# A two-layer attention kernel: layer 1's first projections and rotations as work items of layer 0's last steps, and scores and maxima in strict turns

## Chip, cores and metric

The kernel runs on one core of a Trainium2 chip. The metric is the device time of one launch in microseconds. TensorE is called PE here (PEld: its weight loads), VectorE DVE, ScalarE ACT, GpSimd POOL, and SyncE, which issues the DMAs, SP.

## What is computed

Two layers on x of 2 x 1024 rows of 128 (float32), each `x = x + attention(norm(x)) + ffn(norm(x))`:

```
# layer 0: 16 heads of 8, ALiBi and causal mask, softmax
att = softmax(q @ k.T / sqrt(8) + slope * (j - i), causal);  y = (att @ v) @ W_proj + b_proj
# layer 0 ffn: second normalisation, input quantised by one global maximum, ternary weight
xq = clip(xn2 * 128 / gamma); y = (xq @ w_q) * (gamma * beta / 128)
# layer 1: 16 query heads of 64 over 4 key heads, rotary embedding, linear attention
q, k = rope(xn @ Wq.T), rope(xn @ Wk.T)
per chunk: o = ((q k^T) * decay) v + (q * q_dec) state;  state = blk_dec * state + (k * k_dec)^T v
# layer 1 ffn: linear plus top-2 of 8 experts of rank 4
```

`rope(x) = x * cos + rotate_half(x) * sin`.

## The kernel before

**Layer 0.** Groups of four heads, eight groups (two batches by four), ten steps each: steps 0 to 79. Step `s` has unit `u = s % 10` of group `n = s // 10`: a block of scores up to 512 columns wide for each of four heads (256 in u = 2 and 9), its exponential on ACT (line 1480), the zeroing of the upper triangle in diagonal blocks on POOL (`affine_select`, 1620), and one step later the product with V (`pv`, 721), which adds in PSUM bank 7. ACT copies the sum to `yacc` twice in a group (1469). Scores rotate over three banks (`ST_BANKS`), so that a head's score waits for the exponential of the head three before.

**Items.** The softmax needs the row maxima of the same scores one group ahead. For each group there are 18 maxima items: PE makes a block of scores for a pair of heads (`max_piece`, 591, one product in rows 0 to 63 of the array and one in rows 64 to 127 for the two heads, in up to two pieces, and `max_done`, 605, which adds the causal mask by 64 x 64 products in nine of eighteen or so), DVE reduces (1170). All items share two pairs of banks: item k waits until item k - 2 has been used (`used(pe, k - 2)`). `item_stream` lists the items in order, `MIDWAY` puts those of the attention's finish between the maxima, and `TAIL` gives those after the last maxima a step of their own. `items_of_step(s)` deals two paced items to a step. Per step PE runs, for each half (heads 0, 1, then 2, 3): scores and half of the items, and after both halves `pv(s - 1)`. DVE runs the step's items in their order, and after them what is put at that step by name: `LN1_STEP` (moments, inverse root and normalisation of batch 0 for layer 1: one after the item `back` of span 1), `QUANTISE_STEP`, `ternary` and so on.

**The finish** of a span of 512 rows is `yt` (two a span, heads back to rows and division), `yT`, `proj` (659, 661: ffn product and projection in one bank, DVE adds the bias, 1183), `back` (665, DVE adds to x, 1220); then `xn1T` turns the normalised rows of batch 0 for layer 1 (680, 1192). Before the change these fall in steps 42, 45, 49, 52 (`yt`), 56, 59 (`yT`), 68, 71 (`proj`), 72, 73 (`back`), 76 (`xn1T`); the normalisation is at step 74.

**Hand-over.** Spans 2 and 3 (batch 1) are finished after step 79 by the list `POST`: eight `turn_heads` (800), `yT`, `proj`, `back`. The ten projections of layer 1's first span (`("p", 0, m)`: two of keys, eight of queries, 836) stand between them. A projection is rotated so: DVE multiplies by cos (1313) into `kr` or `qr`, and by sin (1317) into one of three slots of `by_sin`; SP waits for it and issues two DMAs (521) that swap odd and even rows into one of four slots of `turned`; POOL adds that to `kr` or `qr` (1641). After POST: `chunk_vk(0)` (844, 847), ACT's copy of `vk` and eight `vdec` (1501, 1512), `scores1(0)` (865), which needs the rotated keys and queries, then per chunk `kv_sums` (919), the next span's projections, `mix` (889) and `carry` (906).

Of `scores_beside`, which the change rewrites, this is the core before:

```
for odd in (1, 0):
    scores(s, [heads[1 - odd]])
    if odd:
        used(pe, k - 2)
        max_ready(k)
    for t in range(len(ROUNDS[...])):
        last = max_piece(k, t, odd)
max_done(k, last)
```

Of the kernel before, what the change touches and what calls it, by code (L numbers as in the profile page):

```python
# [78 lines left out]
for _name, _n in [("cos", T), ("sin", T), ("decay", H1 * D1), ("qdec", QT * P), ("kdec", H1),  # L79
# [67 lines left out]
ITEM_AT_TURN = TURN_AT[0, 0]  # L147
ITEM_AT = {(kind, n): k for k, (kind, n, u) in enumerate(ITEMS) if u == 0}
# [29 lines left out]
QUANTISE_STEP = [63, 65]  # L178
# [4 lines left out]
def build(nc, x, w, wright, consts, alibi_q, alibi_k, masks, chosen, out):  # L183
    alibi_q, alibi_k, masks, chosen = (v.bitcast(BF16) for v in (alibi_q, alibi_k, masks, chosen))
    with ExitStack() as ctx:
# [71 lines left out]
        qr = sb("qr", [P, 2, QT, SPAN], F32, l1)
        kr = sb("kr", [P, 2, 2, SPAN], F32, l1)

        apart = sb("apart", [P, 6 * T], F32, l1)  # L260
        qd = sb("qd", [P, 2, QT, P], F32, l1)
        state = sb("state", [P, STATES, QT, D1], F32, l1)
# [102 lines left out]
        POST = []  # L365
# [6 lines left out]
        PJ = [("p", 0, m) for m in range(PROJ)]  # L372
# [68 lines left out]
        def _(sp):  # L441
# [69 lines left out]
            def turn_halves(i, ms):  # L511
# [27 lines left out]
        def _(pe):  # L539
# [32 lines left out]

            def max_ready(k):
# [21 lines left out]
            def max_done(k, last):  # L595
# [16 lines left out]
            def scores_beside(s, heads, k):  # L612
                for odd in (1, 0):
                    scores(s, [heads[1 - odd]])
                    if odd:
                        used(pe, k - 2)
                        max_ready(k)
                    for t in range(len(ROUNDS[MAX_OF[ITEMS[k][2]][1]])):
                        last = max_piece(k, t, odd)
                max_done(k, last)  # L620

            def item(k):
# [20 lines left out]
                elif kind != "turn":  # L643
# [129 lines left out]
            for s in range(NSTEP + 1):  # L773
                beside = items_of_step(s) if s < NSTEP else ()
                for half in range(2):
                    mine = (beside[:(len(beside) + 1) // 2], beside[(len(beside) + 1) // 2:])[half]
                    if s < NSTEP:
# [4 lines left out]
                        else:  # L782
                            scores(s, heads)
# [46 lines left out]
            def project1(i, ms):  # L830
# [3 lines left out]
                for m in ms:  # L834
                    w = W["k1"][:, P * m:P * m + P] if m < 2 else W["q1"][:, P * (m - 2):P * (m - 2) + P]
                    mm(bank01(("p", i, m)), w, xnT[:, SPAN * i:SPAN * i + SPAN], start=True, stop=True).then_inc(s_pj, 1)  # L836

            def chunk_vk(c):
# [7 lines left out]
                for pr in range(2):  # L846
                    last = tr(ps[:, KV1 * D1 + P * pr:KV1 * D1 + P * pr + P], kr[:, i % 2, pr, P * ch:P * ch + P], W["ident"])  # L847
# [3 lines left out]
            def scores1(c):  # L851
# [5 lines left out]
                for pr in range(2):  # L857
# [158 lines left out]
        def _(v):  # L1016
# [231 lines left out]
            def after_attention():  # L1248
                v.wait_ge(s_big, 48)
                for name in POST:  # L1250
# [49 lines left out]
            def rope(i, ms):  # L1300
# [3 lines left out]
                for m in ms:  # L1304
                    n = PROJ * i + m
# [5 lines left out]
                    t = slice(SPAN * (i % 2), SPAN * (i % 2) + SPAN)  # L1311
                    dst = kr[:, i % 2, m, :] if m < 2 else qr[:, i % 2, m - 2, :]
                    note(vec.tensor_tensor(dst, ps, K["cos"][:, t], ALU.mult))  # L1313
                    if n >= SIN_SLOTS:
                        q, slot = divmod(n - SIN_SLOTS, TURN_SLOTS)
                        v.wait_ge(s_turned[slot], 32 * (q + 1))
                    vec.tensor_tensor(by_sin[:, n % SIN_SLOTS, :], ps, K["sin"][:, t],  # L1317
                                      ALU.mult).then_inc(free(("p", i, m)), 1)
# [8 lines left out]
            def fade_q(c):  # L1327
# [4 lines left out]
                vec.tensor_tensor(qd[:, c % 2, :, :], qr[:, i % 2, :, P * ch:P * ch + P],  # L1332
# [228 lines left out]
        def _(g_):  # L1561
# [46 lines left out]

            for s in range(NSTEP):
# [22 lines left out]

            def rotate(i, ms):

                if i == NSPAN:
                    return
                for m in ms:
                    n = PROJ * i + m
                    g_.wait_ge(s_turned[n % TURN_SLOTS], 32 * (n // TURN_SLOTS + 1))
# [130 lines left out]
```

## Time and profile before

| | us |
|---|---|
| median of three runs (lowest, highest) | 517.77 (517.55, 519.68) |
| the profiled execution | 513.83 |
| its span | 512.0 |
| mean granted clock | 0.944 |

The profile tells of one execution. Times of instructions are from the start of its span. The granted clock is a share of 2.4 GHz: 1.00 or 0.50 at a time, in between over a longer stretch. A releaser behind `<-` is what ended an engine's idle time, and the idle time stands before it.

### The profile page before, as it was taken

Reading aid. Unit: us, or ns where it says so; the run is one execution under the profiler, and the core shown is the slowest. Engines: PE = TensorE matmul, PEld = TensorE weight load, DVE = VectorE, ACT = ScalarE, POOL = GpSimd, SP = SyncE. Lnnn points to the kernel's source line nnn. Section 1 sums busy time; section 2 is a strip of 40 time slices with the busy share of each in tenths; the row PEclk is TensorE's granted clock in tenths of the full one; section 3 lists DMA queues with packets and bytes.
Section 4 is the critical chain, followed back from the end, with each engine's and each line's share of the span. In section 5 each row is a group of like instructions: output and inputs, shape, how many; then the busy total and the mean of one; then the engine's idle time right before and its main releaser. Section 6 shows DMA issues by size and latency. Waiting matters only on the chain. (4 is left out here: it accounts for less than half of the span.)

```text
span 512.0 us, 10900 instructions
## 1 busy us (share of the span) xinstructions
PE 434.6 (85%) x4283; PEld 199.5 (39%) x4284; DVE 354.2 (69%) x612; ACT 264.9 (52%) x593; POOL 183.6 (36%) x277
## 2 busy tenths in 40 slices
PE   6797989898998989998886796959698769889995
PEld 3253223232332323332221342426274526446764
DVE  5878778878898788888825485885908690777351
ACT  2566387877776677768577212435313530453331
POOL 3013425354322204132220165649307830685220
PEclk9999599999999899999999897987989997998999
DMA  7542070424202020020000031220102210120000
GB/s 238 191 125 71 8 241 2 173 50 170 70 3 69 2 59 14 3 70 2 2 3 2 10 139 57 104 73 32 63 22 79 69 61 22 63 83 2 3 22 22
DMA packets 19094, 31.95 MB, mean 62 GB/s; under 512 B 2544, under 2 KB 7120, under 8 KB 18724
## 3 DMA queue, kind: packets, MB, share of 16 engines
q1 hardware_dynamic: 19044, 31.27, 18.8%
q8 instruction: 34, 0.56, 0.4%
q14 instruction: 16, 0.13, 0.1%
HBM read 13.23 MB, written 8.06 MB: 42 GB/s over the span
## 5 line engine op out<-in xcount | busy, mean ns | idle before, releaser
L1170 DVE TENSOR_REDUCE pmax<-PS 128x8 f32<-128x1024 f32 x144 | 170.7, 1220 | 39.0 <-PE PS L605 30.0
L1480 ACT ACTIVATE prob<-PS 128x512 f32<-128x512 f32 (+1 forms) x320 | 158.3, 560 | 68.8 <-PE PS L703 67.0
L703 PE MATMUL PS<-q_op,k_op 55*128 55x512 bf16 (+3 forms) x384 | 93.0, 335 | 12.4 <-ACT prob L1480 10.0
L1620 POOL TENSOR_SCALAR_AFFINE_SELECT prob<-prob 128x512 f32<-128x512 f32 x64 | 39.9, 635 | 165.2 <-ACT prob L1480 165.2
L591 PE MATMUL PS<-k_op,q_op 52*128 52x512 bf16 (+3 forms) x384 | 80.1, 343 | 11.6 <-DVE pmax L1170 8.6
L721 PE MATMUL PS<-prob,vaug 128*16 128x512 f32 (+3 forms) x768 | 81.1, 512 | 1.8 <-ACT prob L1480 1.8
L703 PEld LDWEIGHTS PS<-q_op,k_op 55*128 55x128 bf16 x384 | 26.1, 95 | 87.9 <-ACT prob L1480 69.6
L1658 POOL TENSOR_TENSOR xn<-state,c_sb 128x512 f32<-128x512 f32 x28 | 32.1, 1147 | 77.7 <-DVE state L1350 69.0
L836 PE MATMUL PS<-xnT,w_sb 128*128 128x512 f32 x80 | 43.9, 648 | 14.4 <-DVE by_sin L1317 14.4
L1350 DVE TENSOR_TENSOR state<-PS,xn 128x512 f32<-128x512 f32 x28 | 19.3, 688 | 45.7 <-PE PS L919 34.1
L1641 POOL TENSOR_TENSOR qr<-qr,turned 128x512 f32<-128x512 f32 x32 | 43.0, 1361 | 5.0 <-DMA turned<-by_sin 4.9
L937 PE MATMUL PS<-oT,w_sb 128*128 128x256 f32 (+1 forms) x160 | 33.5, 372 | 1.2 <-ACT oT L1547 1.2
L1547 ACT COPY oT<-PS 128x512 f32<-128x512 f32 x32 | 17.2, 588 | 32.6 <-PE PS L906 32.5
L591 PEld LDWEIGHTS PS<-k_op,q_op 52*128 52x128 bf16 x384 | 21.7, 95 | 30.3 <-DVE pmax L1170 22.6
L1512 ACT ACTIVATE vdec<-vk,c_sb 128x64 f32<-128x64 f32 x128 | 32.3, 334 | 0.5
L1501 ACT COPY vk<-PS 128x512 f32<-128x512 f32 x16 | 9.3, 584 | 44.0 <-PE PS L847 44.0
L937 PEld LDWEIGHTS PS<-oT,w_sb 128*128 128x128 f32 x160 | 28.4, 210 | 8.6 <-issue 3.7
L1317 DVE TENSOR_TENSOR by_sin<-PS,c_sb 128x512 f32<-128x512 f32 x40 | 27.1, 679 | 0.0
L1313 DVE TENSOR_TENSOR qr<-PS,c_sb 128x512 f32<-128x512 f32 x32 | 21.9, 684 | 7.5 <-PE PS L836 7.4
L865 PE MATMUL PS<-qr,kr 64*64 64x256 f32 x256 | 19.7, 416 | 8.6 <-POOL qr L1641 8.6
L1324 DVE TENSOR_TENSOR sm<-PS,c_sb 128x512 f32<-128x512 f32 x32 | 20.5, 680 | 9.1 <-PE PS L865 9.1
L1332 DVE TENSOR_TENSOR qd<-qr,c_sb 128x1024 f32<-128x1024 f32 x16 | 24.8, 1547 | 0.0
(186 smaller groups left out, 533.7 us busy)
## 6 DMA issues: line engine op xcount, KB each, us to landing
turned<-by_sin SPq DMA_DIRECT2D x80, 128.0 KB, 2.0
k_op<-k_scr SPq DMA_DIRECT2D x14, 220.0 KB
q_op<-q_scr SPq DMA_DIRECT2D x14, 208.0 KB
c_sb<-const_dram SPq DMA_DIRECT2D x1, 2060.0 KB, 7.2
w_sb<-w_dram SPq DMA_DIRECT2D x1, 1876.5 KB, 7.8
q_scr<-part_a SPq DMA_DIRECT2D x6, 256.0 KB, 3.5
k_scr<-part_a SPq DMA_DIRECT2D x6, 256.0 KB, 3.7
q_scr<-part_b SPq DMA_DIRECT2D x6, 256.0 KB, 3.4
```

The lines of the kernel that those rows point to most:

```text
L591: return mm(PS[:, ring + odd, P * at:P * (at + nb)], q_op[rows, slot, pair, P * i:P * i + P], k_op[rows, slot, pair, P * j:P * (j + nb)], ...
L703: last = mm(PS[:, (GH * s + h) % ST_BANKS, at:at + nn], k_op[rows, slot, h // 2, P * j:P * j + P], q_op[rows, slot, h // 2, P * i0:P * i0 ...
L721: last = mm(PS[STRIP * h:STRIP * h + VW, 7, c0:c0 + nn], vaug[:, TPB * b + j, g * GH + h, :], prob[:, s % P_SLOTS, h, at:at + nn], start=( ...
L836: mm(bank01(("p", i, m)), w, xnT[:, SPAN * i:SPAN * i + SPAN], start=True, stop=True).then_inc(s_pj, 1)
L937: last = mm(of_half(ps, s), wo[:, C * kt:C * kt + C], of_half(oT[:, i % 2, kt, :], s), start=False, stop=(chunks.stop == TPS and s == 1 an ...
L1170: vec.tensor_reduce(pmax[:, of_pair, at:at + TPS], both.rearrange("p a (b c) -> p a b c", c=P), AX.X, ALU.max).then_inc(done, 1)
L1317: vec.tensor_tensor(by_sin[:, n % SIN_SLOTS, :], ps, K["sin"][:, t], ALU.mult).then_inc(free(("p", i, m)), 1)
L1480: sca.activation(prob[:, s % P_SLOTS, h, 0:UNIT_W[u]], PS[:, k % ST_BANKS, 0:UNIT_W[u]], ACT.Exp).then_inc(s_exp, 1)
L1512: sca.mul(vdec[:, c % 2, g, h % HPG, :], vk[:, c % 2, D1 * g:D1 * g + D1], K["kdec"][:, h:h + 1]).then_inc(s_vd_a, 1)
L1620: po.affine_select(out=blk, in_=blk, compare_op=ALU.is_ge, fill=0.0, base=0, pattern=[[0, GH], [1, P]], channel_multiplier=-1).then_inc(s_ ...
L1641: po.tensor_tensor(dst, dst, turned[:, n % TURN_SLOTS, :], ALU.add).then_inc(done, 1)
L1658: po.tensor_tensor(faded, state[:, u % STATES, :, :], fade, ALU.mult).then_inc(s_faded, 1)
```

## The change

Nothing of what is computed changes. Five things are altered.

1. The finish of batch 0 is placed earlier. By `item_stream` the steps are now: `yt` 42, 44, 46, 47; `yT` 49, 51; `proj` 52, 54; `back` 56, 57; `xn1T` 63. `LN1_STEP` follows `back` of span 1: step 58. `QUANTISE_STEP` is 48 and 50, not 63 and 65.
2. A new item `p1` makes two projections of layer 1's first span into the two banks of the item's pair, and DVE multiplies both by cos and sin. The five stand in steps 70, 72, 73, 75 and 76. SP waits for the item; POOL adds the swapped rows at the end of steps 72, 74, 75, 77, 78, after that step's `affine_select`. `POST` holds no projection any more.
3. `scores_beside`: the second head's score comes after all products of the maximum, masks included; these alternate between the two halves of the array's rows.
4. In other steps the two heads of a half have their scores one after the other, each with its own wait.
5. `qr` and `kr` are two tensors each, and the buffers of layer 1 lie in another order, so that the first span's and `by_sin` and `turned` can be written while layer 0 still runs.

```diff
+APART = 6848
-TAIL = [(71, "proj", 1, 0), (72, "back", 0, 0), (73, "back", 1, 0), (76, "xn1T", 0, 0)]
-MIDWAY = {(5, 5): ("yt", 0, 0), (5, 11): ("yt", 0, 1), (6, 0): ("yt", 1, 0), (6, 6): ("yt", 1, 1),
-          (6, 12): ("yT", 0, 0), (7, 0): ("yT", 1, 0), (7, 17): ("proj", 0, 0)}
+MIDWAY = {(5, 6): ("yt", 0, 0), (5, 9): ("yt", 0, 1), (5, 12): ("yt", 1, 0), (5, 15): ("yt", 1, 1),
+          (6, 0): ("yT", 0, 0), (6, 3): ("yT", 1, 0), (6, 6): ("proj", 0, 0), (6, 9): ("proj", 1, 0),
+          (6, 12): ("back", 0, 0), (6, 15): ("back", 1, 0), (7, 8): ("xn1T", 0, 0)}
+TAIL = [(70, "p1", 0, 0), (72, "p1", 0, 1), (73, "p1", 0, 2), (75, "p1", 0, 3), (76, "p1", 0, 4)]
+TURN_STEP = {72: 0, 74: 1, 75: 2, 77: 3, 78: 4}
...
-QUANTISE_STEP = [63, 65]
+QUANTISE_STEP = [48, 50]
...
-        for i, ms in zip(SECOND, (range(0, 3), range(0))):
-            POST += [("yt", i, g) for g in range(NG)] + [("p", 0, m) for m in ms]
         i, j = SECOND
-        POST += [("yT", i), ("p", 0, 3), ("p", 0, 4), ("proj", i), ("yT", j), ("p", 0, 5), ("back", i), ("p", 0, 6),
-                 ("proj", j), ("p", 0, 7), ("back", j), ("p", 0, 8), ("p", 0, 9)]
+        POST = [("yt", i, g) for g in range(NG)] + [("yt", j, g) for g in range(NG)]
+        POST += [("yT", i), ("proj", i), ("yT", j), ("back", i), ("proj", j), ("back", j)]
...
-                    freed(sp, ("p", i, m))
+                    if i:
+                        freed(sp, ("p", i, m))
+                    else:
+                        used(sp, P1_AT[m // 2])
...
-                        for odd in range(2):
+                        for odd in (1, 0):
                             rows = slice(HALF * odd, HALF * odd + HALF)
...
             def scores_beside(s, heads, k):
-                for odd in (1, 0):
-                    scores(s, [heads[1 - odd]])
-                    if odd:
-                        used(pe, k - 2)
-                        max_ready(k)
-                    for t in range(len(ROUNDS[MAX_OF[ITEMS[k][2]][1]])):
+                scores(s, heads[0:1])
+                used(pe, k - 2)
+                max_ready(k)
+                for t in range(len(ROUNDS[MAX_OF[ITEMS[k][2]][1]])):
+                    for odd in (1, 0):
                         last = max_piece(k, t, odd)
                 max_done(k, last)
+                scores(s, heads[1:2])
...
+                    elif kind == "p1":
+                        pe.wait_ge(s_big, 48)
+                        used(pe, ITEM_AT["xn1T", 0])
+                        for m in (2 * u, 2 * u + 1):
+                            last = mm(o[:, m % 2, :], weights_of(m), xnT[:, 0:SPAN], start=True, stop=True)
...
-                            scores(s, heads)
+                            for h in heads:
+                                scores(s, [h])
...
+                elif kind == "p1":
+                    v.wait_ge(s_big, 48)
+                    for m in (2 * u, 2 * u + 1):
+                        ins = rotated(0, m, both[:, m % 2, :])
...
+            def rotated(i, m, ps):
+                n = PROJ * i + m
+                t = slice(SPAN * (i % 2), SPAN * (i % 2) + SPAN)
+                dst = kr[i % 2][:, m, :] if m < 2 else qr[i % 2][:, m - 2, :]
+                note(vec.tensor_tensor(dst, ps, K["cos"][:, t], ALU.mult))
+                if n >= SIN_SLOTS:
+                    q, slot = divmod(n - SIN_SLOTS, TURN_SLOTS)
+                    v.wait_ge(s_turned[slot], 32 * (q + 1))
+                return vec.tensor_tensor(by_sin[:, n % SIN_SLOTS, :], ps, K["sin"][:, t], ALU.mult)
...
+                if s in TURN_STEP:
+                    rotate(0, range(2 * TURN_STEP[s], 2 * TURN_STEP[s] + 2))
...
-            rotate(0, range(PROJ))
```

## Rows read from the trace of the kernel before

**Rows 1.** The page, part 1: busy us, share of the span, instructions.
```profile
PE 434.6 (85%) x4283; PEld 199.5 (39%) x4284; DVE 354.2 (69%) x612; ACT 264.9 (52%) x593; POOL 183.6 (36%) x277
```
**Rows 2.** Stages: length, busy PE, PEld, DVE, ACT, POOL, PEclk, DMA share, GB/s.
```profile
82.40:106.00 23.60, 21.60 (x207) 6.57 (x202) 19.67 (x18) 19.34 (x40) 9.76 (x21) 1.00 0.37 121
169.20:175.10 5.90, 4.89 (x37) 1.69 (x37) 3.18 (x4) 3.43 (x8) 1.25 (x3) 0.71 0.01 2
314.00:326.00 12.00, 12.00 (x113) 5.58 (x110) 9.94 (x15) 3.53 (x11) 4.45 (x5) 0.82 0.17 61
```
**Rows 3.** Timeline, steps 16 and 17: start, length, instruction, idle before.
```profile
97.95 0.39 PE L703 MATMUL PS<-q_op,k_op 55*128 55x512 bf16 x1
...
99.41 0.11 PEld L605 LDWEIGHTS PS<-masks_sb 64*64 64x64 bf16 x4 [0.23 <-issue]
...
100.57 0.39 PE L703 MATMUL PS<-q_op,k_op 55*128 55x512 bf16 x1
...
101.25 2.36 DVE L1170 TENSOR_REDUCE pmax<-PS 128x8 f32<-128x1024 f32 x2 [0.26 <-PE PS L591]
...
102.03 1.05 PE L721 MATMUL PS<-prob,vaug 128*16 128x512 f32 x8
...
103.01 0.33 PE L703 MATMUL PS<-q_op,k_op 55*128 55x384 bf16 x1
```
**Rows 4.** The page, part 5: busy, mean ns, idle before, most of it for.
```profile
L1170 DVE TENSOR_REDUCE pmax<-PS 128x8 f32<-128x1024 f32 x144 | 170.7, 1220 | 39.0 <-PE PS L605 30.0
L1480 ACT ACTIVATE prob<-PS 128x512 f32<-128x512 f32 (+1 forms) x320 | 158.3, 560 | 68.8 <-PE PS L703 67.0
```
**Rows 5.** Timeline of the hand-over.
```profile
287.17 0.58 ACT L1469 COPY yacc<-PS 128x512 f32<-128x512 f32 x1 [2.58 <-PE PS L721]
...
288.81 0.26 DVE L1212 RECIPROCAL rden<-PS 128x16 f32<-128x16 f32 x1 [11.12 <-PE PS L800]
...
312.98 1.13 PE L865 MATMUL PS<-qr,kr 64*64 64x256 f32 x8 [3.70 <-POOL qr L1641]
...
314.03 0.30 PEld L919 LDWEIGHTS PS<-vdec,vk 64*64 64x64 f32 x8 [0.74 <-POOL vdec L1649]
```
**Rows 6.** Timeline, first and last part of the normalisation on DVE.
```profile
267.63 1.64 DVE L1039 BATCH_NORM_STATS2 stats<-x_sb 128x6 f32<-128x128 f32 x8
...
273.08 2.14 DVE L1058 TENSOR_SCALAR xn<-x_sb,mv,rstd 128x128 f32<-128x128 f32 x8
```
**Rows 7.** Timeline, items of the finish in steps 71, 73 and 76.
```profile
259.97 1.12 PE L659 MATMUL PS<-xn2T,w_sb 128*128 128x512 f32 x2
...
261.89 0.39 PE L703 MATMUL PS<-q_op,k_op 55*128 55x384 bf16 x4
...
266.14 0.66 PE L665 MATMUL PS<-w_sb,sT 128*128 128x128 f32 x4
...
276.47 1.22 DVE L1192 COPY xnT<-PS 128x1024 f32<-128x1024 f32 x1 [1.25 <-PE PS L680]
```
**Rows 8.** Timeline of steps 40 and 41.
```profile
167.15 0.28 DVE L1140 TENSOR_SCALAR xn<-w_sb,small 128x128 f32<-128x128 f32 x1
...
169.79 0.39 PE L687 MATMUL PS<-masks_sb,mpart 128*12 128x128 bf16 x4 [0.83 <-DVE pmax L1170]
...
171.74 1.91 PE L721 MATMUL PS<-prob,vaug 128*16 128x512 f32 x8
```
**Rows 9.** Timeline of steps 75 to 79.
```profile
272.20 0.39 PE L703 MATMUL PS<-q_op,k_op 55*128 55x512 bf16 x2 [0.83 <-ACT prob L1480]
...
275.37 1.06 PE L680 MATMUL PS<-w_sb,xn 128*128 128x128 f32 x8 [1.47 <-DVE xn L1058]
...
282.99 1.22 POOL L1620 TENSOR_SCALAR_AFFINE_SELECT prob<-prob 128x512 f32<-128x512 f32 x2 [1.90 <-ACT prob L1480]
...
284.67 0.63 POOL L1620 TENSOR_SCALAR_AFFINE_SELECT prob<-prob 128x512 f32<-128x512 f32 x1 [0.46 <-ACT prob L1480]
```
**Rows 10.** The tile `turned`: length ns min/median/max; DMAs to landing.
```profile
L521 SPq DMA_DIRECT2D turned<-by_sin x80: 464/590/1474, 292.6 to 454.8; - x80
L1641 POOL TENSOR_TENSOR kr<-kr,turned x8: 1267/1271/1280, 295.3 to 442.0; 128x512 f32<-128x512 f32 x8
...
DMA to landing us min/median/max: 1.9/2.0/3.7
```

More of the change, by code:

```diff
@@ L147 @@
 ITEM_AT_TURN = TURN_AT[0, 0]
+P1_AT = {u: k for k, (kind, n, u) in enumerate(ITEMS) if kind == "p1"}
 ITEM_AT = {(kind, n): k for k, (kind, n, u) in enumerate(ITEMS) if u == 0}
@@ L253, in build @@
         sm = sb("sm", [P, 4, SPAN], F32, l1)
+        qr1, kr1 = sb("qr1", [P, QT, SPAN], F32, l1), sb("kr1", [P, 2, SPAN], F32, l1)
+        state = sb("state", [P, STATES, QT, D1], F32, l1)
+        apart = sb("apart", [P, APART], F32, l1)
+        qd = sb("qd", [P, 2, QT, P], F32, l1)
+        qr0, kr0 = sb("qr0", [P, QT, SPAN], F32, l1), sb("kr0", [P, 2, SPAN], F32, l1)
         by_sin = sb("by_sin", [P, SIN_SLOTS, SPAN], F32, l1)
         turned = sb("turned", [P, TURN_SLOTS, SPAN], F32, l1)
[L257 to L262, printed above, removed]
+        qr, kr = (qr0, qr1), (kr0, kr1)
         l1.close()
@@ L363, in build @@
             RA += [("yT", i), ("proj", i)]
-        POST = []
-        for i, ms in zip(SECOND, (range(0, 3), range(0))):
-            POST += [("yt", i, g) for g in range(NG)] + [("p", 0, m) for m in ms]
         i, j = SECOND
-        POST += [("yT", i), ("p", 0, 3), ("p", 0, 4), ("proj", i), ("yT", j), ("p", 0, 5), ("back", i), ("p", 0, 6),
-                 ("proj", j), ("p", 0, 7), ("back", j), ("p", 0, 8), ("p", 0, 9)]
-        PJ = [("p", 0, m) for m in range(PROJ)]
+        POST = [("yt", i, g) for g in range(NG)] + [("yt", j, g) for g in range(NG)]
+        POST += [("yT", i), ("proj", i), ("yT", j), ("back", i), ("proj", j), ("back", j)]
+        PJ = []
         NORM_CHUNK, TURN_CHUNK = 1, 3
@@ L571, in _, with weights_of @@
             pe.wait_ge(s_masks, 16)
+            def weights_of(m):
+                return W["k1"][:, P * m:P * m + P] if m < 2 else W["q1"][:, P * (m - 2):P * (m - 2) + P]
             def max_ready(k):
@@ L834, in project1 @@
                 for m in ms:
[L835 to L836 removed]
+                    mm(bank01(("p", i, m)), weights_of(m), xnT[:, SPAN * i:SPAN * i + SPAN], start=True, stop=True).then_inc(s_pj, 1)
             def chunk_vk(c):
@@ L846, in chunk_vk @@
                 for pr in range(2):
-                    last = tr(ps[:, KV1 * D1 + P * pr:KV1 * D1 + P * pr + P], kr[:, i % 2, pr, P * ch:P * ch + P], W["ident"])
+                    last = tr(ps[:, KV1 * D1 + P * pr:KV1 * D1 + P * pr + P], kr[i % 2][:, pr, P * ch:P * ch + P], W["ident"])
                 last.then_inc(s_pj, 1)
@@ L865, in scores1 @@
                             last = mm(PS[half_of(s), 2 + q, 256 * pr:256 * pr + 256].rearrange("p (a t) -> p a t", a=HPG),
-                                      kr[rows, i % 2, pr, t], qr[rows, i % 2, HPG * pr:HPG * pr + HPG, t],
+                                      kr[i % 2][rows, pr, t], qr[i % 2][rows, HPG * pr:HPG * pr + HPG, t],
                                       start=True, stop=True, skip_group_check=True)
@@ L1185, in item @@
                     add_to_x(n, both[:, 0, :]).then_inc(done, 1)
+                elif kind == "p1":
+                    v.wait_ge(s_big, 48)
+                    for m in (2 * u, 2 * u + 1):
+                        ins = rotated(0, m, both[:, m % 2, :])
+                        if m % 2 == 0:
+                            note(ins)
+                    ins.then_inc(done, 1)
                 elif kind == "lanes":
@@ L1310, in rope @@
                         v.wait_ge(s_sc, 2 * TPS * (i - 1))
[L1311 to L1318, printed above, removed]
+                    rotated(i, m, ps).then_inc(free(("p", i, m)), 1)
             def masked(c, q):
@@ L1331, in fade_q @@
                     v.wait_ge(s_o, 2 * (c - 1))
-                vec.tensor_tensor(qd[:, c % 2, :, :], qr[:, i % 2, :, P * ch:P * ch + P],
+                vec.tensor_tensor(qd[:, c % 2, :, :], qr[i % 2][:, :, P * ch:P * ch + P],
                                  K["qdec"].rearrange("p (k t) -> p k t", k=QT), ALU.mult).then_inc(s_qd, 1)
@@ L1607, in normalise_again, with rotate @@
                 po.tensor_scalar(xn[:, j, :], xn[:, j, :], rstd2[:, j:j + 1], None, ALU.mult).then_inc(s_xn2, 1)
+            def rotate(i, ms):
+                if i == NSPAN:
+                    return
+                for m in ms:
+                    n = PROJ * i + m
+                    g_.wait_ge(s_turned[n % TURN_SLOTS], 32 * (n // TURN_SLOTS + 1))
+                    dst, done = (kr[i % 2][:, m, :], s_kr) if m < 2 else (qr[i % 2][:, m - 2, :], s_qr)
+                    po.tensor_tensor(dst, dst, turned[:, n % TURN_SLOTS, :], ALU.add).then_inc(done, 1)
             for s in range(NSTEP):
@@ L1631, in _ @@
             po.memset(state[:, 0, 0, :], 0.0).then_inc(s_zero, 1)
[L1633 to L1639, printed above, removed]
-                    dst, done = (kr[:, i % 2, m, :], s_kr) if m < 2 else (qr[:, i % 2, m - 2, :], s_qr)
-                    po.tensor_tensor(dst, dst, turned[:, n % TURN_SLOTS, :], ALU.add).then_inc(done, 1)
             def fade_v(c):
```

5 lines of the change are left out of this document (removed).

## The prediction

> **What bounds the kernel now.** Order of reading: busy shares and costly groups of the page, a stretch of clean steps, one step at close range, then the places that the diff touches. By the page PE is busy 85% and DVE 69% [rows 1]; neither is a bound by itself. In 82.4 to 106.0, nine clean steps of layer 0, PE has 21.60 us of work in 23.6, DVE 19.67, ACT 19.34 [rows 2].
>
> The close view of steps 16 and 17 [rows 3] shows a loop, not a full engine: score of head 0 at 100.57, its exponential, head 3's score when that has freed a bank, P·V at 102.03, and head 0 of the next step at 103.01: 2.44 us. Step 16 (97.95 to 100.57), with a mask product between head 3's score and P·V, is 2.62: the mask costs 0.18. DVE needs 2.36 for a step's two maxima, ACT about 2.1 for four exponentials and up to 0.6 more where it copies. So a step has three limits close together. The page says the same: ACT stands idle 68.8 us before exponentials, nearly all for scores, and DVE 39.0 before maxima, 30.0 of it for items that end in a mask [rows 4].
>
> After layer 0 it is a chain: the last accumulator copy starts at 287.17 (0.58 long) and layer 1's first state product at 314.03, 26.3 us after the copy's end [rows 5]. In it lie eight head turns, ten projections and their rotations on DVE, SP's queue and POOL.
>
> **1. The normalisation at step 58.** It follows `back` of span 1, now an item of step 57. The block runs on DVE from 267.63 to 275.22 without a break, 7.6 us [rows 6]. There it hid beside an idle DVE; at 58 it stands ahead of the maxima of steps 59 and 60, and PE can be only two items ahead (the item pair of banks). By step 17's spacing, DVE is done with an item about 0.7 us before PE asks for its banks: 7.6 - 0.7 = 6.9 us of stall. Bounds: 7.6 (no slack), and 3.3, if DVE regains its idle time of the clean stretch (3.9 us in nine steps, 4.3 by step 68). I take 6.9, since two items are all that the banks hold.
>
> **2. The rest of batch 0's finish, in steps 42 to 63.** New in loaded steps are the second `proj`, two `back` and `xn1T`. `proj` holds PE from 259.97 to 261.89, 1.92 us; `back` 0.66 and some 0.3 of change around it; `xn1T` has 1.22 on DVE, where little room is left [rows 7]. I take 1.9 + 2 x 0.95 + 1.0 = 4.8; bounds 2.3 (each fills idle time of 0.8, as PE has in the last steps) and 6. The head turns, `yT`, the first `proj` and both quantising passes move among steps of equal load: 0, bounds -1 and +1.5.
>
> **3. PE's clock after the stall.** The nearest row is a small one: in step 40 a DVE chain of 1.4 us from 167.15 makes PE wait 0.83 for it, and then the clock is 0.71 over 5.9 us, which is half speed for 3.4 of them; P·V takes 1.91 instead of 1.05 [rows 2, 3, 8]. Half speed for 3.4 us loses 1.7, with the waits it moves 2.0. A hole of 7 us is larger than that one. I take +2.0, bounds 0 and 4. The Trainium skill (TensorE: Matmul & The Clock Gate, "The HAM clock gate") says that the chip gates PE's clock to half after idleness and releases it under work. By that rule the drop is certain, by the row it is likely; the term is the same.
>
> **4. Strict turns.** Where a half's first item is a maximum, all its products and masks now stand ahead of the second head's score. So the second item's masks leave the stretch from head 3 to P·V, 0.18 in steps 1, 5, 6, 8 and 9 of ten, but DVE (2.36) and ACT take over close behind: 0.1 in some 30 steps, -3. Against that, the first item's masks (steps 0, 2, 3 and 9) put the second head's score from 0.2 to about 0.7 us after the first, and ACT could be 0.2 late where it has no slack: 15 steps x 0.1, +1.5. I take -1.5, bounds -6 (0.1 in nearly all 66 steps) and +5 (0.2 in 26 steps). A mask's loads stand 0.23 behind the products before them [rows 3]. The Trainium skill (TensorEngine Tiling (Array Packing), "Key Properties") says that a change of tiling mode drains the engine. By that rule a mask ahead of head 3 adds a change back, and this term would be about +1.
>
> **5. Steps 70 to 79.** Five `p1` items, each two fp32 products as `proj` has: 1.92. PE stands idle 0.83 before the second pair of scores in a plain step [rows 9], so each adds 1.1: +5.5. Gone are `proj` and two `back` (1.92 + 2 x 0.66, less 0.83 in two steps: 1.6) and `xn1T` with its wait for the normalisation (1.06 + 1.47 - 0.83 = 1.7 [rows 9]), and in plain steps each head's score now waits for itself, 0.1 x 7. Net +1.5. The transfers: SP issues twenty at 0.59 in 25 us, behind nothing but the last `mrow` loads, 2.0 to landing [rows 10]. DVE has four operations, 2.5 us, an item, less than such a step is long, beside idle time. If that cover fails (three slots of `by_sin`, each freed by a landing), the steps wait: bounds -1 and +6.
>
> **6. POOL at the end.** The rotations of projections 8 and 9 stand at step 78, after its fills. DVE ends item 4 some 3.5 us after step 76 starts; the transfers land 2.7 and 4 us later; POOL adds twice, 1.27 each [rows 10], between the fills of step 78 (282.99, 1.22) and that of 79 (284.67) [rows 9], on which P·V waits. Fill 79 could have started 0.4 to 0.8 after those of 78; behind 2.5 it is 1.7 late: +1.7, bounds 0 and 3.
>
> **7. Hand-over.** Left after the last copy: eight head turns (DVE from 1.1 us after the copy [rows 5], 0.62 each, done after 6.1), then `yT`, `proj`, `sT`, `back` for two spans, interleaved, one after another's product at 0.6, 1.0, 0.7, 0.6 and 0.7 for the addition: 12.0. Then `vk` 1.0, its copy 0.6, eight `vdec` 2.0 and semaphores: the state product 15.9 after the copy, not 26.3: -10.4. The wait of 3.70 for POOL's rotated queries [rows 5] is gone too; late next is ACT's `vdec`. Bounds -8 and -13. In 314 to 326 the clock is 0.82, half speed for 4.3 us, behind that wait [rows 2]; if PE's holes shrink, up to 2.2 comes back: I take -1.0.
>
> Sum: 6.9 + 4.8 + 2.0 - 1.5 + 1.5 + 1.7 - 10.4 - 1.0 = +4.0. The profiled execution took 513.83 (span 512.0), so one like it would take 517.8; the median of the runs is 517.77, 3.94 more, and 4.0 on that is 521.8.
>
> **Rivals.** *DVE is fed early and catches up* (faster). If strict turns hand it the second maximum ahead of head 3's wait in every step, the 39 us of idle time before maxima [rows 4] shrink, part 4 is -4.5, DVE regains 3.6 of the block at 58, and PE's hole is too short for the clock: 4.0 - 3.0 - 3.6 - 2.0 = -4.6, 513.2. It decides where that idle time falls under half. Against it: the loop of 2.44 holds no maximum.
> *The clock stays up* (no change): no drop at 59, and strict turns give 2.5 more: 4.0 - 2.0 - 2.5 = -0.5, 517.3. For it: clock stretches depend on where in a pause they fall. Against: step 40.
> *The rotation ring holds the last steps* (slower still): DVE waits in `by_sin` for a landing, the item banks stay full, part 5 is at its bound of +6: 526.3. For it: the same ring fills in the hand-over now. Against: mostly two steps between items.
> That the projections do not leave the hand-over is excluded: no wait ties the items to the last copy.
>
> Chances: forecast 0.43, ring 0.12, clock up 0.23, DVE catches up 0.22. A measurement tells 0.5%, 2.6 us, from no change. So slower 0.55, same 0.23, faster 0.22. Range 511 to 528, the forecast's own 519 to 525.
>
> **What would show it.** Right: DVE's block at step 58 with a hole of 6 to 7 us in PE and a stretch at half clock behind it; the last copy about 15 us later than now; the state product some 16 us after it. Wrong: no hole in steps 59 to 61; clean steps below 2.4; the last copy before 295, or the state product 20 or more behind it.

## The result, and the profile after

The changed kernel takes 538.0 us (median of four runs, 532.79 to 540.18), the one before 517.66 (four runs, 514.21 to 519.68): ratio 1.045, interval 1.040 to 1.050. The direction was as forecast, the size was not: +4 forecast, 20 to 23 measured, and outside the range. Time below is compared by ratio where experiments are set against each other; 1% is 5.16 us. A ratio, and a half-speed time below, is taken over the runs within 1.5% of the fastest of their kernel, a median over all of its runs, and the two differ by up to 0.6% (this kernel is at 1.045 by the first and at 1.039 by the second, or 1.043 against 29 later runs of the kernel before).

The page of the changed kernel, beside [rows 1] and [rows 4]: busy times, the granted clock in 40 slices (before it was 0.944 in the mean, here 0.899), and the two groups of the layer 0 loop.
```profile
PE 460.7 (86%) x4283; PEld 206.9 (38%) x4284; DVE 355.7 (66%) x612; ACT 267.6 (50%) x593; POOL 184.8 (34%) x277
...
PEclk9997599959999698897698978796989997998999
...
L1501 ACT ACTIVATE prob<-PS 128x512 f32<-128x512 f32 (+1 forms) x320 | 160.1, 559 | 95.1 <-PE PS L718 93.9
L1183 DVE TENSOR_REDUCE pmax<-PS 128x8 f32<-128x1024 f32 x144 | 171.2, 1221 | 53.7 <-PE PS L615 42.2
```
PE is busy 26 us longer with as many instructions (4283), while ACT and DVE have the same work and more idle time, most of it for PE. So PE ran slower: the clock, not more work on another engine.

Stages of the changed kernel, cut at the first exponential of steps 4, 19, 41, 49, 60, 69, 70 (columns as in [rows 2]). The windows begin at those steps and end at steps 19, 23, 43, 52, 64, 70 and 79.
```profile
67.17:105.77 38.60, 36.42 (x336) 10.98 (x336) 31.67 (x29) 31.79 (x66) 13.82 (x29) 1.00 0.37 123
105.77:124.20 18.43, 17.12 (x128) 5.96 (x128) 9.91 (x11) 8.42 (x19) 7.72 (x17) 0.63 0.23 79
175.96:187.78 11.82, 10.52 (x65) 3.73 (x65) 6.48 (x10) 4.03 (x10) 3.25 (x9) 0.57 0.00 1
206.46:220.52 14.06, 11.96 (x100) 4.47 (x98) 11.10 (x13) 7.10 (x14) 5.36 (x11) 0.76 0.01 2
247.21:270.45 23.24, 16.00 (x116) 4.90 (x116) 16.90 (x38) 9.52 (x20) 4.00 (x10) 0.63 0.01 2
282.90:288.05 5.15, 2.60 (x25) 1.04 (x26) 0.40 (x2) 1.77 (x6) 2.74 (x8) 0.85 0.01 2
288.05:316.39 28.34, 25.93 (x145) 7.59 (x145) 12.42 (x20) 19.03 (x39) 12.66 (x13) 0.97 0.25 94
```
The same cuts in the kernel before, without step 69:
```profile
67.42:106.07 38.65, 35.37 (x338) 10.71 (x337) 32.27 (x29) 31.31 (x66) 13.99 (x29) 1.00 0.38 127
106.07:118.17 12.10, 11.20 (x129) 4.78 (x129) 9.33 (x10) 7.73 (x19) 7.53 (x17) 1.00 0.10 22
169.18:177.99 8.81, 7.78 (x66) 2.94 (x66) 5.95 (x10) 4.21 (x10) 2.10 (x5) 0.81 0.00 1
194.59:203.45 8.86, 8.62 (x101) 3.73 (x98) 7.13 (x10) 6.30 (x15) 3.28 (x10) 1.00 0.01 2
228.01:238.67 10.66, 9.68 (x106) 3.25 (x103) 8.28 (x8) 8.53 (x20) 3.69 (x9) 1.00 0.00 1
257.75:283.11 25.36, 18.33 (x144) 5.89 (x144) 10.37 (x44) 19.47 (x39) 3.49 (x7) 1.00 0.01 2
```
At full clock the strict order changes nothing: steps 4 to 18 take 38.60, before 38.65. The last copy to `yacc` ends 35.1 us later than before (322.90 against 287.76). Of that, steps 60 to 63 give 12.6, steps 19 to 22 give 6.3 (equal work, clock 0.63 instead of 1.00), steps 49 to 51 5.2, steps 41 and 42 3.0, steps 70 to 78 3.0, the rest 5.0 together. Then the hand-over gives 8.8 back.

Timeline of the changed kernel: the normalisation, the hole, and what follows. Start, length, instruction, idle before.
```profile
245.08 1.65 DVE L1052 BATCH_NORM_STATS2 stats<-x_sb 128x6 f32<-128x128 f32 x8
...
250.54 2.14 DVE L1071 TENSOR_SCALAR xn<-x_sb,mv,rstd 128x128 f32<-128x128 f32 x8
...
253.87 0.61 PE L601 MATMUL PS<-k_op,q_op 52*128 52x256 bf16 x4 [6.76 <-DVE pmax L1183]
255.41 1.82 ACT L1501 ACTIVATE prob<-PS 128x512 f32<-128x512 f32 x3 [7.60 <-PE PS L718]
...
260.43 1.91 PE L736 MATMUL PS<-prob,vaug 128*16 128x512 f32 x8
```
The hole is there with the forecast length. But P·V still takes 1.91 instead of 1.05, and it starts 6.6 us after PE went on. A window of this kernel and one of the first experiment, which has the old order of products, both after the hole:
```profile
254.00:262.00 8.00, 8.00 (x53) 1.97 (x49) 4.56 (x4) 4.86 (x9) 1.43 (x3) 0.50 0.00 1
```
```profile
243.00:251.00 8.00, 7.83 (x71) 2.43 (x74) 5.18 (x5) 6.01 (x13) 2.13 (x4) 0.70 0.00 1
```
In the strict order PE is busy for all of 8 us and stays at 1.2 GHz; in the old order, no busier, it is back at 2.4 within them. The whole stretch at half clock runs from 249.0 to 266.0. It begins inside the hole, which starts at 247.1, and 12.1 us of PE's work lie in it:
```profile
249.00:266.00 17.00, 12.13 (x83) 3.27 (x83) 11.72 (x24) 6.27 (x13) 2.88 (x6) 0.50 0.01 2
```
In the first experiment it runs from 237.6 to 247.8, and PE goes on at 242.2: 5.6 us of it come behind the hole.

The hand-over of the changed kernel, beside [rows 5]:
```profile
317.98 2.49 POOL L1638 TENSOR_TENSOR qr<-qr,turned 128x512 f32<-128x512 f32 x2
320.43 0.64 POOL L1651 TENSOR_SCALAR_AFFINE_SELECT prob<-prob 128x512 f32<-128x512 f32 x1
321.21 1.05 PE L736 MATMUL PS<-prob,vaug 128*16 128x256 f32 x8 [1.14 <-POOL prob L1651]
322.32 0.58 ACT L1490 COPY yacc<-PS 128x512 f32<-128x512 f32 x1 [4.72 <-PE PS L736]
323.21 5.75 PE L816 MATMUL PS<-w_sb,yacc 128*128 128x128 f32 x32 [0.95 <-issue]
...
340.40 1.99 PE L934 MATMUL PS<-vdec,vk 64*64 64x256 f32 x16 [1.19 <-ACT vdec L1533]
```
The first state product comes 17.5 us after the copy's end, not 26.3. From there to the end nothing changes: 197.84 against 197.92.

### The profile page after: what moved, and what is told of

Read it like the earlier page. It is cut to its first block and busy times, and to the rows that moved or that the text cites. A ratio compares the mean times of both kernels' runs of the same rounds, so it can differ in the third digit from the quotient of the medians.

```text
span 538.2 us, 10867 instructions
## 1 busy us (share of the span) xinstructions
PE 460.7 (86%) x4283; PEld 206.9 (38%) x4284; DVE 355.7 (66%) x612; ACT 267.6 (50%) x593; POOL 184.8 (34%) x277
## 5 line engine op out<-in xcount | busy, mean ns | idle before, releaser
L1501 ACT ACTIVATE prob<-PS 128x512 f32<-128x512 f32 (+1 forms) x320 | 160.1, 559 | 95.1 <-PE PS L718 93.9
L1183 DVE TENSOR_REDUCE pmax<-PS 128x8 f32<-128x1024 f32 x144 | 171.2, 1221 | 53.7 <-PE PS L615 42.2
L718 PE MATMUL PS<-q_op,k_op 55*128 55x512 bf16 (+3 forms) x384 | 97.4, 355 | 5.8 <-ACT prob L1501 3.4
L601 PE MATMUL PS<-k_op,q_op 52*128 52x512 bf16 (+3 forms) x384 | 75.2, 361 | 17.4 <-DVE pmax L1183 13.3
L736 PE MATMUL PS<-prob,vaug 128*16 128x512 f32 (+3 forms) x768 | 86.8, 544 | 2.8 <-POOL prob L1651 2.8
L851 PE MATMUL PS<-xnT,w_sb 128*128 128x512 f32 x60 | 33.8, 663 | 13.6 <-DVE by_sin L1226 13.6
L601 PEld LDWEIGHTS PS<-k_op,q_op 52*128 52x128 bf16 x384 | 20.4, 98 | 34.1 <-DVE pmax L1183 22.9
L1672 POOL TENSOR_TENSOR vdec<-vk,c_sb 128x256 f32<-128x256 f32 x32 | 18.9, 611 | 28.2 <-ACT vk L1522 28.2
L736 PEld LDWEIGHTS PS<-prob,vaug 128*16 128x16 f32 x768 | 15.1, 99 | 32.1 <-issue 23.0
L1345 DVE TENSOR_TENSOR sm<-PS,c_sb 128x512 f32<-128x512 f32 x32 | 20.5, 683 | 6.5 <-PE PS L880 6.5
```

What stands on the lines that cost most here:

```text
L601: return mm(PS[:, ring + odd, P * at:P * (at + nb)], q_op[rows, slot, pair, P * i:P * i + P], k_op[rows, slot, pair, P * j:P * (j + nb)], ...
L718: last = mm(PS[:, (GH * s + h) % ST_BANKS, at:at + nn], k_op[rows, slot, h // 2, P * j:P * j + P], q_op[rows, slot, h // 2, P * i0:P * i0 ...
L736: last = mm(PS[STRIP * h:STRIP * h + VW, 7, c0:c0 + nn], vaug[:, TPB * b + j, g * GH + h, :], prob[:, s % P_SLOTS, h, at:at + nn], start=( ...
L851: mm(bank01(("p", i, m)), weights_of(m), xnT[:, SPAN * i:SPAN * i + SPAN], start=True, stop=True).then_inc(s_pj, 1)
L1183: vec.tensor_reduce(pmax[:, of_pair, at:at + TPS], both.rearrange("p a (b c) -> p a b c", c=P), AX.X, ALU.max).then_inc(done, 1)
L1501: sca.activation(prob[:, s % P_SLOTS, h, 0:UNIT_W[u]], PS[:, k % ST_BANKS, 0:UNIT_W[u]], ACT.Exp).then_inc(s_exp, 1)
```

## The experiments

"Half speed" is the time that PE had 1.2 GHz, worked out for each run as 2 x (1 - granted clock) x span, and averaged over a kernel's runs. The kernel before has 57.4 us of it in the 29 runs beside e1 to e4 (37.7 to 66.8), 57.2 beside e5 to e8 and 62.0 beside e9 to e12; the changed one has 99.6. The first number behind each experiment is its median. A ratio has an interval of about 0.5% either way, so a difference of two ratios is good to some 0.7%, or 4 us. "Strict order" is the order of the change's points 3 and 4.

**e1: the strict order undone.** The changed kernel with the three old places of order:
```
- scores(s, heads[0:1]); used(pe, k - 2); max_ready(k)
- for t in ...: for odd in (1, 0): ...
- scores(s, heads[1:2])
+ for odd in (1, 0):
+     scores(s, [heads[1 - odd]])
+     if odd: used(pe, k - 2); max_ready(k)
+     for t in ...
- for h in heads: scores(s, [h])
+ scores(s, heads)
```


> The changed kernel (median 538.0) with its scores and maxima back in the old order; everything else stays. Theory 'hole' (the normalisation's hole on the vector engine and the longer half-speed stretches behind it are the loss, strict turns are near nothing): 536 to 540, with the half-speed stretch of 17 us behind step 60 still there. Theory 'turns' (the new order starves PE, and causes the added half-speed stretches, as the one from 109.0 to 122.7): 526 to 531, total half-speed time down from 110 us to about 80. My estimate in the prediction was 1.5 us in favour of strict turns, so 539.5.


528.03, ratio 1.0235 (1.018 to 1.029), half speed 66.5. So 2.15%, 11 us, hangs on the order of the products (7 to 15 us with the noise of both).

**e2: the strict order alone.** The reverse edit in the kernel before.


> The kernel before (median 517.7) with strict turns alone. Theory 'hole': 515 to 519, and no more half-speed time than its 59 us. Theory 'turns': 523 to 528, with new half-speed stretches around steps 19 to 22 and 40 to 42.


519.92, ratio 1.0033 (0.999 to 1.008), half speed 59.9. Alone the strict order costs next to nothing (0.8% by the median). The two experiments contradict each other unless the order acts through something else in the changed kernel.

**e3: no normalisation at step 58.** Eight one-column operations stand in its place, so layer 1 reads an `xn` that is not the normalised one.
```
- moments(0); inverse_root(slice(0, TPB), 1e-5); normalise(0)
+ for j in range(TPB):
+     vec.tensor_scalar(xn[:, j, 0:1], x_sb[:, j, 0:1], 1.0, None, ALU.mult)
```


> The changed kernel with the normalisation block of step 58 left out (moments, inverse root, normalisation of batch 0 for layer 1; eight one-column operations stand in its place). Theory 'hole': PE's hole of 6.76 us is gone and with it the 17 us at half speed behind it; steps 60 to 63 last about 12 us, not 23.2: 524 to 528. Theory 'turns': only the hole goes, 531 to 533, since the slower clock has its cause elsewhere.


521.28, ratio 1.0044 (0.999 to 1.009), half speed 56.3. By the ratios the block costs 4.1% in strict order, 21 us, of which only 6.8 are the hole.

**e8: e3 with the old order.** It completes the square.


> The changed kernel in the old order of scores and maxima and with the normalisation block of step 58 left out (eight one-column operations in its place): what is left is the moved finish, p1 and the hand-over. If the two causes add (17 for the block, 10 for the order): 510 to 513. If they overlap, because the order only lengthens the half-speed stretch behind the hole: 518 to 521.


518.78, ratio 1.0050 (1.0015 to 1.009), half speed 58.0. The four corners, as ratios to the kernel before:

| | without the block | with it | the block costs |
|---|---|---|---|
| old order | e8 1.0050 | e1 1.0235 | 1.85%, 9.5 us |
| strict order | e3 1.0044 | changed kernel 1.0450 | 4.06%, 21 us |

By the ratios the order costs nothing without the block and 11 us with it, so that the two together cost more than their sum, by 11 us give or take 5. By the medians the corners are 1.006, 1.023, 1.010 and 1.039; the order then costs 2 us without the block and 8 with it.

The profiled executions say where. The windows of steps 60 to 63, here of e1 and then of e3:
```profile
235.58:256.19 20.61, 12.75 (x116) 4.49 (x116) 16.95 (x39) 9.27 (x20) 3.99 (x10) 0.75 0.01 2
```
```profile
240.83:253.31 12.48, 10.87 (x115) 4.11 (x112) 10.30 (x10) 9.11 (x19) 4.00 (x10) 1.00 0.01 2
```
With the hole in old order PE has 12.75 us of work for the same instructions that take 16.00 in strict order. The wait of the old order is the same, by the timeline of e1, and its P·V is at full speed 5.8 us after the products behind the hole:
```profile
242.24 0.62 PE L601 MATMUL PS<-k_op,q_op 52*128 52x256 bf16 x4 [6.75 <-DVE pmax L1182]
...
248.03 1.05 PE L736 MATMUL PS<-prob,vaug 128*16 128x512 f32 x8
```

In the four corners steps 60 to 63 take 12.38 (e8), 20.61 (e1), 12.48 (e3) and 23.24 us (changed kernel). In place, then, the block costs 8.2 us in the old order and 10.8 in the strict one, and the order makes 2.5 us of difference, not 11. The profiled executions of e1 and of the changed kernel are 11.5 us apart, and 11.7 of that stand ahead of the block: step 58 begins at 230.54 in e1 and at 242.22 in the changed kernel, and from there to the end they take 296.2 and 296.0. In e3 step 58 begins at 235.84. Nothing that DVE does in step 58 can act on the steps ahead of it, and there the changed kernel, e3 and e12 (below) are the same program. Their steps 19 to 57, in this order:
```profile
105.77:242.22 136.45, 124.06 (x1019) 42.74 (x1021) 103.63 (x125) 84.98 (x173) 34.78 (x80) 0.89 0.16 43
106.70:235.84 129.14, 115.67 (x1019) 40.48 (x1021) 103.14 (x125) 84.02 (x173) 34.21 (x80) 0.96 0.16 46
106.60:235.45 128.85, 114.36 (x1019) 39.91 (x1021) 103.00 (x125) 83.91 (x173) 34.23 (x80) 0.97 0.17 46
```
The same 1019 products take PE 8 to 10 us longer in one execution than in the others: 30.7, 10.2 and 6.8 us of these steps are at half clock. So a part of what separates these profiles is a difference between executions of the same code, in which the block has no hand that they show; how much of the 21 and the 11 us it makes cannot be told from one profile of each kernel. What goes with the order is more of such stretches: in steps 19 to 57 the five profiles with the strict order and the moved finish (changed kernel, e3, e4, e6, e12) have 6.8 to 30.7 us at half clock, the other nine 0 to 6.8.

**e6: only the halves without a maximum in the old order.** `for h in heads: scores(s, [h])` is `scores(s, heads)` again, the rest of the change stands.


> The changed kernel (538.0), where only the halves without a maximum have both heads' scores together again; beside a maximum the strict turns stay. If the order beside a maximum is what costs: 535 to 539. If the separate scores of the plain halves do: about 528, as with both undone.


536.17, ratio 1.039 (1.033 to 1.046), half speed 91.0. Its interval overlaps that of the changed kernel and lies above that of e1: what costs is the order in halves with a maximum (`scores_beside`, and the order of the masks in `max_done`). Its steps 60 to 63 take 23.23, as in the changed kernel.

**e10 and e11: the block alone, in the kernel before.** An extra normalisation whose result nobody reads follows step 58, in e10 with the old order, in e11 with the strict one (e2).
```
+ if s == 58:
+     moments(0); inverse_root(slice(0, TPB), 1e-5)
+     for j in range(TPB): note(vec.tensor_scalar(xn[:, j, :], x_sb[:, j, :], ...))
```


> The kernel before (515.6) with a second copy of the normalisation block behind the items of step 58, its result not used: a hole of 7 us and nothing else, in the old order of scores and maxima. The hole alone costs 6.7; with the half-speed stretch behind it 522 to 528, some 8 to 14 us more at half speed.


524.72, ratio 1.0137 (1.007 to 1.020), half speed 64.9, only 3 more than the kernel before beside it.


> The same added block on the kernel before with strict turns (519.9). Theory 'with strict turns the clock comes back later from a hole' (17.1 us at half speed behind step 60 against 10.2 in the old order): 530 to 535, so the block costs 11 to 15 here against 7 to 12 there. Theory 'no interplay': the same surcharge as in the old order, 526 to 529.


531.03, ratio 1.0254 (1.019 to 1.032), half speed 76.5. Steps 58 to 63, e10 and then e11:
```profile
220.41:247.55 27.14, 18.91 (x170) 6.15 (x166) 20.96 (x55) 12.48 (x27) 7.03 (x18) 0.75 0.05 10
```
```profile
221.93:252.41 30.48, 22.53 (x170) 6.64 (x166) 21.23 (x55) 12.97 (x28) 6.99 (x18) 0.66 0.03 7
```
Same instructions, and PE works 3.6 us longer in strict order. Without the block those steps take 17.36 and 17.70, so it costs 9.8 and 12.8 in place, 3.0 apart, as in the changed kernel (2.5). That part of the effect does not need the moved items. By the ratios the block costs 1.37% in the old order and 2.21% in the strict one, 4.4 us apart, which is within the noise of four ratios (5 us).

**e12: the same work in three holes.** Moments at step 58, inverse root at 60, normalisation at 62 (`if s == LN1_STEP + 2`, `+ 4`).


> The changed kernel (538.0) with the normalisation in three parts: moments after step 58 (2.3 us), inverse root after 60 (3.1), normalisation after 62 (2.1). If what matters is the work on the vector engine: still 6 us of waits, no more than 2 better. If it is the length of PE's hole (one of 6.8 us takes the clock down, three of 1.5 to 2.5 do not): 523 to 528.


527.14, ratio 1.0218 (1.016 to 1.028), half speed 76.7. At step 60 PE waits 1.61 us for DVE's maxima, and the clock falls in that wait. Steps 60 to 63 and the largest wait left:
```profile
240.44:260.05 19.61, 15.50 (x115) 4.95 (x117) 17.33 (x38) 9.64 (x20) 4.00 (x10) 0.71 0.01 2
```
```profile
PE PS L695 <- DVE pmax L1183: 2.6, 1, 2.6
```
By the ratios the kernel gains 2.3%, 12 us (8 to 16). The number was forecast by the theory that short holes leave the clock up, but they do not: in steps 60 to 69 it is at half for 16.7 us, against 18.6 in the changed kernel. What the traces show in place is smaller: DVE does the same work in the same steps, steps 60 to 63 take 3.6 us less, and 3.1 of these are PE's idle time (4.1 against 7.2), probably because DVE regains some idle time between the pieces. The rest of the 10.5 us between the two profiled executions stands ahead of step 58 (6.8 us), in the same code.

**e4: the normalisation late.** It stands in step 69, where DVE has time.
```
- (7, 8): ("xn1T", 0, 0)      LN1_STEP = step_of(ITEM_AT["back", 1]) + 1
+ LN1_STEP = NSTEP - NU - 1
- TAIL = [(70, "p1", 0, 0), (72, ..), (73, ..), (75, ..), (76, ..)]
+ TAIL = [(73, "xn1T", 0, 0), (74, "p1", 0, 0), (75, ..), (76, ..), (77, ..), (78, ..)]
+ TURN_STEP = {76: 0, 77: 1, 78: 2}; rotate(0, range(6, PROJ)) after the steps
```


> The changed kernel with the normalisation after step 69, where the vector engine has no maxima left, xn1T in step 73 and the five p1 items in steps 74 to 78 (rotations 6 to 9 after step 79). Theory 'hole': as the run without the block, less 1 for xn1T out of a full step, plus 2 to 3 for a denser end: 524 to 529. Theory 'turns': 530 to 533. If the rotation ring of three slots binds with p1 in five successive steps: 3 to 5 more in steps 75 to 79.


521.71, ratio 1.0054 (1.001 to 1.010), half speed 61.9: as good as without the block.

**e5: e4 with the old order.**


> The changed kernel with the late normalisation of the run before (after step 69, p1 in steps 74 to 78; 521.7) and with scores and maxima in the old order. Theory 'order holds the clock down' (strict turns cost nothing at full speed, but with them PE spends more time at half speed): 515 to 518, with 10 to 25 us less time at half speed. Theory 'only the normalisation's hole makes strict turns dear': no hole here, so 520 to 523 as with them.


514.75, ratio 0.9995 (0.996 to 1.003), half speed 50.4. The strict order costs 0.6% here (0 to 1.1), with no block at step 58.

**e7: only the projections moved.** The kernel before up to step 69, with its order and its places of the finish; eight projections, not ten, in steps 76 to 79, and the normalisation after step 72.
```
TAIL = [(70, "proj", 1, 0), (71, "back", 0, 0), (72, "back", 1, 0), (75, "xn1T", 0, 0),
        (76, "p1", 0, 0), (77, "p1", 0, 1), (78, "p1", 0, 2), (79, "p1", 0, 3)]
TURN_STEP = {79: 0}        # rotate(0, range(2, PROJ)) after the steps
POST: "p" 8 and 9 between yT, proj and back
```


> A combination: the finish of batch 0, the quantising and the order of scores and maxima as in the kernel before up to step 69; then proj in step 70, back in 71 and 72, the normalisation after 72, xn1T in 75 and four p1 items (eight projections) in 76 to 79; projections 8 and 9 and nearly all rotations after the last step. Theory 'the last steps and the hand-over have room, the loaded steps have none': last copy at 288 to 293 instead of 287.8, first state product 18 to 20 after it instead of 26.3: 509 to 513. Theory 'the ring of slots and POOL bind': the state product stays 24 to 26 after the copy, and the time is 517 to 520.


509.6, ratio 0.988 (0.985 to 0.992), half speed 48.2. Its hand-over still waits, in the ring of `by_sin`, since only one pair is rotated before the end:
```profile
293.17 0.69 DVE L1228 TENSOR_TENSOR by_sin<-PS,c_sb 128x512 f32<-128x512 f32 x1 [3.56 <-DMA turned<-by_sin]
...
293.96 5.11 PE L816 MATMUL PS<-w_sb,yacc 128*128 128x128 f32 x32 [3.90 <-DVE by_sin L1228]
```

**e9: e7 with the ring freed earlier.** `TURN_STEP = {77: 0, 79: 1}`, so that POOL adds two pairs in the steps.


> The run with eight projections in the last steps (509.6), with rotations 0 and 1 at step 77 and 2 and 3 at step 79 instead of 0 and 1 at step 79 alone. In that run's trace the vector engine waits 3.56 us in by_sin for a landing that hangs on rotation 0, and PE 3.90 us for it after the last copy. If that ring is on the path: both waits go, 505.5 to 507. If it is hidden: 509 to 510.


504.15, ratio 0.976 (0.971 to 0.982), half speed 39.8: faster than both kernels. Its hand-over:
```profile
283.03 2.50 POOL L1642 TENSOR_TENSOR kr<-kr,turned 128x512 f32<-128x512 f32 x2
...
290.33 0.59 ACT L1494 COPY yacc<-PS 128x512 f32<-128x512 f32 x1 [1.53 <-PE PS L737]
291.27 3.88 PE L816 MATMUL PS<-w_sb,yacc 128*128 128x128 f32 x32 [0.99 <-DVE by_sin L1228]
...
307.67 1.09 PE L934 MATMUL PS<-vdec,vk 64*64 64x256 f32 x16 [1.87 <-ACT vdec L1537]
```
The additions are over before the last copy and nothing waits behind them; the head turns follow it in 3.88 us, at full clock, where the changed kernel needs 5.75. State product 16.75 us after the copy's end. The last copy is only 3.2 later than before, the rest of the kernel 3.1 shorter.

## Why the prediction was wrong in size

In the sum of steps, the square of e1, e3 and e8 gives the measured sizes: the moves without the block +2.6 (e8), the block in old order +9.5, the strict order on top of it +11.1; together +23.2. These are sizes by ratio, each good to about 4 us; the profiles place them only in part. The prediction had -3.4 (steps 2, 5, 6 and 7), +8.9 (steps 1 and 3) and -1.5 (step 4).

**Step 1, the stall: right.** 6.9 forecast, 6.76 in the trace, for the reason given: two item banks and DVE's row of maxima behind the block.

**Step 3, the clock after the stall: this is the step that failed.** It held +2.0, with 4 as its upper end, from one row: step 40 of the kernel before, in the old order, with a hole of 0.83; and the sum has no term for the clock anywhere else in layer 0. Behind the stall the clock costs 1.4 us in the old order (8.2 in place, less 6.75 of hole) and 4.0 in the order that the change brings (10.8 less 6.8), its upper end. The rest stands where the sum had nothing: steps 19 to 22 are 6.3 longer, steps 41 and 42 3.0, and steps 49 to 51 take 2.0 more than in e3. These 11 us are half of the 22 by which the profiled execution misses the sum (26.3 longer than the one before, for 4.0). Over the runs half speed is 99.6 us in the mean, against 56.3 without the block; by the ratios the block costs 21 us, 14 beside the hole, so that 43 us more at half speed go with those 14, 0.3 each. In steps 19 to 22, 6.3 us are lost in a stretch of 13.7, 0.46 each. That an idle PE loses its clock is also what the Trainium skill says (TensorE: Matmul & The Clock Gate, "The HAM clock gate"); the trace agrees, the clock falls at 249.0 within the hole that starts at 247.1. The error was to take the length of the slow stretch from a small hole, to price the clock at one place alone, and to hold steps 3 and 4 for independent terms. The row itself was partly chance: e10 has the same code there, and its steps 41 and 42 take 7.47 at full clock, not 8.81.

**Step 4, the strict order: right on what it argued, wrong as a sum.** In clean steps it is worth 0.05 us in fifteen, less than the 1.5 forecast, and e2 shows 0.3%, within the noise. The Trainium skill (TensorEngine Tiling (Array Packing), "Key Properties") says that a change of tiling mode drains the engine; the strict order moves such changes, and no run shows a net price of that (38.60 against 38.65 in steps 4 to 18). What it costs, 11 us by the ratio with e1 and outside the bounds of -6 and +5 that this step gave, comes with the clock: 2.5 us behind the hole, the rest in the profiles ahead of step 58.

**Step 2, the rest of the finish: too small.** From step 43 to 69 e8 takes 8.0 us more than the kernel before, against 4.8:
```profile
178.46:236.71 58.25, 50.95 (x448) 18.03 (x446) 47.05 (x64) 36.43 (x74) 11.38 (x27) 0.97 0.12 32
236.71:266.23 29.52, 24.64 (x239) 8.14 (x236) 21.31 (x20) 21.49 (x45) 7.40 (x19) 1.00 0.01 2
```
```profile
177.99:228.01 50.02, 45.59 (x432) 16.13 (x430) 42.01 (x49) 35.75 (x75) 11.91 (x31) 1.00 0.15 37
228.01:257.75 29.74, 25.70 (x233) 7.82 (x230) 22.72 (x23) 21.45 (x45) 7.10 (x18) 1.00 0.01 2
```
The first pair of rows is e8 (steps 43 to 59, 60 to 69), the second the kernel before. Steps 43 to 59 got 5.0 us of DVE's work and 5.4 of PE's, and are 8.2 longer, with 3.4 us at half clock in them (before none); the emptied steps after them gave back only 0.2. One reason is that the `proj` taken out of step 68 had filled a time in which PE otherwise waits; now it does, in the trace of the changed kernel:
```profile
285.45 0.38 PE L702 MATMUL PS<-masks_sb,mpart 128*12 128x128 bf16 x4 [2.64 <-POOL mpart L1618]
```
That what is taken out of a step may have been free was not in the sum.

**Steps 5 and 6: near enough.** Steps 70 to 78 are 3.0 longer (1.5 forecast, bounds -1 and 6), the end 1.9 (1.7 forecast): the trace shows POOL's two additions for 2.49 right ahead of the last fill, as step 6 said. The ring did not hold the last steps.

**Step 7, the hand-over.** -8.8 against -10.4 and -1.0: the forecast chain is there, but a stretch at half speed from 317.2, 10.2 us long, lies across its head turns (5.75 us, 3.88 in e9). The clock gave nothing back later.

**The rivals.** DVE fed early: no; DVE's idle time before maxima rose from 39.0 to 53.7. Clock stays up: no. Ring: not in the steps; it was in e7's hand-over.

**What stays open.** Why the clock comes back later in the strict order is not settled: PE's busy share does not explain it (8.00 of 8.00 at 0.50, against 7.83 of 8.00 at 0.70), and which half of the order counts was narrowed only to the halves with a maximum. Nor is it settled how much of the 21 us of the block, and of the 11 us of the order, is a matter of which executions were caught: the four of the changed kernel have 89 to 109 us at half speed, and e6, with the same block, 88 to 115, but the one profile of each is longer than that of e3 ahead of step 58 too, by 6.4 and 4.2 us. The stretch at step 19 starts where PE waits for a load, 1.41 us in the changed kernel,
```profile
107.08 0.39 PE L601 MATMUL PS<-k_op,q_op 52*128 52x512 bf16 x2 [1.41 <-DMA k_op<-k_scr]
```
and 0.85 in the kernel before. The seven profiles with the strict order have 1.19 to 1.50 there, the seven with the old one 0.85 to 1.02. Of the first seven four have a stretch in steps 19 to 22 (13.7, 10.2, 3.4 and 3.4 us), of the others none; so the strict order makes this wait longer and the stretch more likely, but the wait of 1.39 in e11 has none behind it and that of 1.27 in e6 has.

## What to carry to other kernels

Don't price a new hole in PE's work by its length alone: put beside it the clock that follows it, and take the row for that from a hole as long, in the same order of instructions; if there is none, the upper end of the range has to be wide. Ask the same for every short wait that a reordering makes longer. Before adding a long block to a loaded engine, look for a place where its reader's banks have slack, or cut the block: by the ratios the same work cost 21 us in one piece at step 58 (10.8 in place), some 9 in three (7.1 in place), and about nothing at step 69. Where several edits come in one change, try them apart and together; here one was nearly free alone and cost 11 us beside another. And before a difference between two kernels is put down to an edit, compare their profiles in the part that the edit cannot touch: here that part alone differed by 6.4 us.

## What the hardware showed that was not expected

- PE at 100% busy stayed at half clock: 254.0 to 262.0 us, 8.00 of 8.00 busy at 0.50. The stretch began 1.9 us into a hole of 6.76 and ended 12.1 us after PE went on.
- The order of small products, with the same instructions and nearly the same hole, goes with how long the half clock lasts: 13.7 us in e10 and 20.5 in e11, by their profiles; 10.2 in e1, 17.1 in the changed kernel and in e6.
- The length of a wait alone does not tell what the clock does: it fell within one of 1.61 us in e12, and stayed up behind one of 1.39 at step 19 of e11.
- The same code can have very different clocks: 30.7, 10.2 and 6.8 us at half speed in steps 19 to 57 of the changed kernel, e3 and e12.
- Time at half speed is most of what one kernel's runs differ by: 37.7 to 66.8 us of it in 29 runs of the kernel before, whose times go from 511.66 to 518.35. Within one kernel a us at half speed goes with 0.2 to 0.5 us of time.
